# Moving 31 layer-norm applications from the vector engine to GpSimd in a software-pipelined transformer kernel

## The reference

```
m = silu(cond) @ w_ada + b_ada            # nine vectors of 256 per batch
x += g1 * self_attn(LN(x)*(1+sc1)+sh1)    # norm 1; 8 windows of 128, rolled by 64, 16 heads
x += g2 * topk_cross(LN(x)*(1+sc2)+sh2)   # norm 2; best 16 of 64 context keys
x += g3 * swiglu(LN(x)*(1+sc3)+sh3)       # norm 3; hidden 1024
x += cross_attn(LN(x)*(1+sc4)+sh4)        # norm 4; second layer, all 64 keys
```

## Time and profile before

| what | value |
|---|---|
| median of three runs | 1159.92 us |
| the profiled execution's own time | 1168.25 us |
| span of that execution (first to last instruction) | 1166.5 us |
| mean granted TensorE clock | 0.91 of full speed |
| TensorE / VectorE / ScalarE / GpSimd busy | 82% / 67% / 41% / 18% |
| rolled halves | 205 to 948 us of the span |

### The profile page before, as it was taken

One profiled execution on the slowest core, in us unless ns is written; L12 is line 12 of the kernel. 1 busy time (PEld: TensorE's weight loads), 2 busy tenths in 40 slices (PEclk: granted clock), 3 DMA queues, 4 the chain that ended last, 5 costly groups with the idle time before them and its releaser, 6 DMA issues.

```text
span 1166.5 us, 23085 instructions
## 1 busy us (share of the span) xinstructions
PE 958.5 (82%) x8080; PEld 690.3 (59%) x8080; DVE 778.3 (67%) x3968; ACT 473.7 (41%) x789; POOL 207.8 (18%) x159
## 2 busy tenths in 40 slices
PE   5886647989888987998899879988898876867976
PEld 4663435577656754676567655775577554733752
DVE  5345785797679854887588746985698748772222
ACT  0232324643455344525463445425552634323312
POOL 0010320411041302201040304110321303010110
PEclk8788868999999998989999999999999997878886
DMA  9360001100010101000100121000101010000000
GB/s 310 124 207 19 10 1 38 29 1 1 20 33 1 46 22 59 28 1 2 37 15 1 47 63 36 10 2 2 51 1 41 7 41 2 1 1 18 1 1 19
DMA packets 29475, 39.36 MB, mean 34 GB/s; under 512 B 4512, under 2 KB 25120, under 8 KB 28848
## 3 DMA queue, kind: packets, MB, share of 16 engines
q1 hardware_dynamic: 29360, 37.85, 9.8%
HBM read 28.34 MB, written 9.50 MB: 32 GB/s over the span
## 4 chain that ended last, share of the span: by engine, by line
PE 60%; DVE 21%; ACT 8%; issue 7%; DMA 2%; SPq 1%; POOL 1%; DVEq 0%; ACTq 0%; POOLq 0%
PE bank L1183 56%; DVE left L1051 7%; DVE top L1049 4%; DVE negm L1015 3%; DVE negm L1080 2%; PE bank L1256 1%; ACT arena L807 1%; ACT arena L781 1%; ACT hT L712 1%; PE bank L1399 1%; DMA qk<-in_rows 1%; DVE arena L1073 1%; DVE xh L895 1%; DVE oT L1029 1%; DMA out<-x 1%
## 5 line engine op out<-in xcount | busy, mean ns | idle before, releaser
L1183 PE MATMUL bank<-w_m,arena 128*128 128x256 f32 x512 | 119.2, 396 | 4.3 <-issue 4.3
L596 POOL TENSOR_SCALAR veps<-mv 128x4 f32<-128x4 f32 (+1 forms) x33 | 7.9, 240 | 603.7 <-DVE mv L890 603.7
L1183 PEld LDWEIGHTS bank<-w_m,arena 128*128 128x128 f32 x512 | 101.4, 200 | 20.8 <-issue 5.8
L636 POOL TENSOR_TENSOR eS<-arena,top 128x1024 f32<-128x1024 f32 x32 | 62.0, 1936 | 239.1 <-DVE top L1049 239.1
L1051 DVE MATCH_REPLACE8 left<-top,arena 128x64 f32<-128x64 f32 x512 | 99.9, 210 | 0.0
L1051 DVE MATCH_REPLACE8 left<-top,left 128x64 f32<-128x64 f32 x512 | 99.8, 209 | 0.0
L762 ACT ACTIVATE arena<-bank 128x512 f32<-128x512 f32 x128 | 66.1, 602 | 64.9 <-PE bank L1183 64.9
L797 ACT ACTIVATE rden<-bank,chan 128x512 f32<-128x512 f32 x64 | 44.1, 689 | 109.3 <-PE bank L1183 109.2
L1183 PE MATMUL bank<-qr,w_m 128*128 128x512 f32 x256 | 86.0, 418 | 1.2 <-ACT qr L720 1.1
L1183 PE MATMUL bank<-h_low,w_m 128*128 128x512 f32 x256 | 73.5, 406 | 15.7 <-DVE h_low L1066 15.1
L1015 DVE TENSOR_REDUCE negm<-bank 128x4 f32<-128x512 f32 x128 | 78.6, 683 | 8.2 <-PE bank L1183 8.2
(11 more groups left out here) (116 smaller groups left out, 1928.3 us busy)
## 6 DMA issues: line engine op xcount, KB each, us to landing
w_m<-in_w_m SPq DMA_DIRECT2D x4, 1024.0 KB, 5.2
kbd<-keys_by_head SPq DMA_DIRECT2D x8, 512.0 KB, 3.5
arena<-in_w_ada SPq DMA_DIRECT2D x1, 2304.0 KB
xin<-in_x SPq DMA_DIRECT2D x4, 512.0 KB, 4.2
arena<-in_w_m SPq DMA_DIRECT2D x1, 2048.0 KB, 11.0
out<-x SPq DMA_DIRECT2D x4, 512.0 KB, 2.9
gate<-gate_rows SPq DMA_DIRECT2D x12, 128.0 KB, 3.6
gated_bias<-gate_rows SPq DMA_DIRECT2D x12, 128.0 KB, 4.1
```

The lines of the kernel that those rows point to most:

```text
L636: nc.gpsimd.tensor_tensor(eS[:], S[:, t, :].rearrange("p (h n) -> p h n", h=H), top[:, :, 0:1].to_broadcast([P, H, LC]), ALU.subtract).the ...
L1183: return nc.tensor.matmul(dst, lhsT, rhs, start=start, stop=stop)
```

## The change

GpSimd's new function `normalise(n, blk, reader)` calls `layer_rstd(n)`, waits for its own `s_rstd[n]`, waits for the reader of `xh`, and issues the four `tensor_scalar` instructions of the block itself. It stands where `layer_rstd(n)` stood. VectorE's `normalise` and its four calls are gone. The context rows and the first block, which are normalised ahead of the pipeline, stay on VectorE. TensorE, ScalarE and the DMA queue are unchanged.

```diff
@@ block.gpsimd, half(st)
+                def normalise(n, blk, reader):
+
+                    layer_rstd(n)
+                    src = xin[:] if n == 1 else x[:, blk]
+                    pool.wait_ge(s_rstd[n], st.blocks(AHEAD_OF[n] if n != 2 else 2, 1, 1))
+                    if reader:
+                        filled_wait(pool, reader, st)
+                    hold(pool)
+                    for t in range(W):
+                        nc.gpsimd.tensor_scalar(xh[:, t, :], src[:, t, :], mv[:, n, t, 0:1], rstd[:, n, t:t + 1],
+                                                ALU.subtract, ALU.mult).then_inc(s_xh[n], 1)
...
                 if front and (st.phase, st.h) != (FILLING, 0):
-                    layer_rstd(1)
-                if back:
-                    layer_rstd(3)
+                    normalise(1, a, ("T", 2, c, KC - 1) if middle else None)
+                if back:
+                    normalise(3, b, ("T", 1, a, KC - 1) if front else ("T", 2, c, KC - 1) if middle else ("T", 4, 0, KC - 1))
...
                 if back:
-                    layer_rstd(4)
+                    normalise(4, b, ("T", 3, b, KC - 1))
                     add_bias(4, b)
...
                 if front:
-                    layer_rstd(2)
+                    normalise(2, a, ("T", 4, b, KC - 1) if back else ("T", 1, a, KC - 1))
@@ block.vector, half(st)
-                def normalise(n, blk, reader):
-
-                    dve.wait_ge(s_rstd[n], st.blocks(2 if n == 2 else AHEAD_OF[n], 1, 1))
-                    if reader:
-                        filled_wait(dve, reader, st)
-                    normalise_tiles(n, xh, xin[:] if n == 1 else x[:, blk], W)
...
-                if front and (st.phase, st.h) != (FILLING, 0):
-                    normalise(1, a, ("T", 2, c, KC - 1) if middle else None)
-                if back:
-                    normalise(3, b, ("T", 1, a, KC - 1) if front else ("T", 2, c, KC - 1) if middle else ("T", 4, 0, KC - 1))
...
-                if back:
-                    normalise(4, b, ("T", 3, b, KC - 1))
...
-                    normalise(2, a, ("T", 4, b, KC - 1) if back else ("T", 1, a, KC - 1))
```

## The result

The changed kernel took 1184.37 us (median of four runs, 1179.23 to 1185.65) against 1159.95 us for the kernel before: a ratio of 1.0194, 95% interval 1.0151 to 1.0238, so clearly slower, by about 2%. The prediction had the sign right and the size wrong: 1166.1 us, range 1158.5 to 1170.0. Its rival (c), a slow tile, is what happened.

What follows compares the result with a forecast made beforehand. The prediction took the chain to be mostly matmul (56% of the span), with normalisation 1%. Rolled -0.5, draining +2.6 and filling +4.1 gave +6.2 us on the median 1159.92: 1166.1 us, range 1158.5 to 1170.0.

Steps and rivals of the forecast that it cites:

- rival (c): GpSimd tile far dearer than its size says, 1.5 us: +35, about 1195 us; decides from 0.99 us a tile; chance 0.07.
- The tile price: One 128x256 tensor_scalar on GpSimd: 0.55 us, from half the two-input addition's slope; upper end 0.78; group of four 2.2 us.
- The draining term: Two draining halves, no cover: three TensorE waits for a normalised tile each grow 0.87 us, +2.6 us in all.
- The filling term: Second filling half: VectorE's cast and subtraction and GpSimd's deviation and norm 2 exclude each other, +4.1 us.
- Rival (a): Second filling half: VectorE does not hold GpSimd up, so -2.1 us there and 1159.9 us in all; chance 0.22.
- Rolled halves: Six halves where other work was to cover GpSimd's longer groups; only a gain of 0.5 us taken in all.
- Norm 2: Rolled halves: 11.7 us of cover before the transposes need it, so the longer group costs nothing.
- norm 3: Rolled halves: 7 us of cover before the transposes; later GpSimd work still in time, so no cost and no gain.
- norm 4: Rolled halves: 4.7 us of cover for a 2.2 us group, gone at 1.17 us a tile; -0.5 us taken.
- VectorE's relief: Rolled halves: VectorE, freed of 1.38 us, starts window divide 0 at most 0.2 us sooner, waiting for ScalarE's denominators.
- rival (b): Rolled halves at norm 4: window divide 0 starts once VectorE is free, gaining 1.38 us a half; chance 0.08.
- Norm 1: Rolled halves: GpSimd done by 461.5, transposes come at 463.24, so no cost; cover gone at 0.99 us a tile.

Runs made afterwards that it cites:

- e11_drain: The changed kernel with norms on GpSimd only in the two draining halves, VectorE normalising elsewhere; 1174.21 us, ratio 1.012 to the kernel before.

## Why the prediction was wrong

**The tile price: wrong, and the step that failed.** "I take half the slope" assumed that one tensor input costs half of two, and it left out that this instruction does two operations for each element. It measured 3.3 ns an element where the two-input addition has 2.14, so neither my 0.55 us nor my upper end 0.78 held; the tile is 1.22, and every group 4.84 instead of 2.2 us. The four-element row could not show a slope, and my range for an unseen operation ended at the dearest neighbour. The Trainium skill ("GPSIMD Engine Reference", section "Elementwise — side-by-side cycle accounting") gives 1.8 cycles for its best loop, from which my estimate was 0.62 us a tile; the trace disagrees, and the measurement decides.

**The draining term: right mechanism, mis-sized.** Three waits, each growing by the group's extra length: at 4.84 us a group, and 0.24 us for GpSimd's wait for itself (0.21 us more than before, where I had 0.05), each is 3.7 us, 11 in all. The traces show these 3.7 us at each of them; the times of e11_drain have 14.4. I had 2.6.

**The filling term: right mechanism.** Exclusion both ways, +4.1 us foretold, +5.7 by the landmarks and +5.9 by the times; the longer group, 2.6 us, more than covers the difference. Rival (a) falls. The argument had one weak place. It gave two kinds of VectorE instruction that exclude GpSimd, those at double rate and those with two inputs, and said that the rows agree. But VectorE's instruction that stood still in the earlier trace rows has one tensor input, and at 0.33 us for 256 elements, 1.3 ns each, it does not run at the cast's rate of 0.56 ns. It was of neither kind, and was held up all the same.

**Rolled halves.** Norm 2, norm 3, norm 4: no cost, as foretold, though at norm 4 the cover of 4.7 us was just used up. VectorE's relief gained at most the 1 us or so foretold (-0.8 +- 1.1 and -0.9 +- 1.0 at equal clock), not rival (b)'s 1.38 us a half. Norm 1: I gave the point, 0.99 us a tile, and stood on the wrong side of it; six times 0.86 us.

**Rival (c)** was the case, between its threshold and its 1.5 us. The prediction's own terms with the measured price are 5.3 for norm 1, -0.5 for norm 4, 4.1 + 2.6 for the filling and 11 for the draining halves, 22.5 us of the 24.5. It had a chance of 0.07, and the range left it out. What should have widened it stood in the text: the power, 1.02 us for four elements against 0.233 for the addition of eps on four, was a row that showed a GpSimd operation several times dearer than size said.

**The measure of no change.** I said 0.2%; single runs of the kernel before spread over 19 us, 1.6%.

## What to carry to other kernels

Before moving an operation to another engine, find its price there in its own form; if no row has it, put the cover of each place beside the price and see how far the price may rise until the first cover breaks. In a software pipeline most places have cover, but the filling and draining parts have none: three of the four draining groups cost more here than all six rolled halves. And where TensorE's clock varies between runs, split a change into parts, repeat what is near zero, and compare the same stretch in several traces rather than the whole of one pair.

## What the runs showed of the hardware

- GpSimd's `tensor_scalar` with two operations on float32 costs 3.3 ns an element and 0.2 to 0.4 us fixed; two wide `tensor_tensor` with repeated operands do the same normalisation in less time.
- VectorE's cast (0.56 ns an element) and its subtraction with two inputs (1.08 ns) hold GpSimd up for as long as they run: 2.07 us for a 0.24 us instruction, 5.17 us for a 1.03 us one.
- The draining part of one and the same order of work took 204.6 to 204.9 us in four traces and 198.5 and 198.7 us in two, with granted clocks of 0.78 and 0.90 in the stretch that differs most.
- The same program had 1151 to 1170 us over 29 runs, with a mean granted clock of 0.934 to 0.909; two sessions of 12 runs of one kernel had mean clocks of 0.915 and 0.921.
